# Keys spread over heads by activations instead of transfers, and a new order of the steps, in a two-layer attention and mixture kernel

## The chip, the cores and the metric

The kernel runs on one core of one Trainium2 chip. The metric is the time of one execution on the device, in microseconds. A core has a matrix engine (PE), a vector engine (DVE), a scalar engine (ACT), GpSimd (POOL), and SyncE (SP), which here issues the transfers. Each runs its own instruction stream in order; they wait for each other by semaphores.

## The reference

The input is 16 images of 64 x 64 pixels with 64 features. Four blocks follow each other, each added to its input, except that the last adds only to the tokens that it chose:

```python
# 1: attention over the 16 images, at each pixel
zn = layernorm(z)
q, k, v = (zn @ W).reshape(n, l, l, H=8, C=16) for Wq, Wk, Wv
g = sigmoid(zn @ Wg + bg)
att = softmax(einsum('iabhc,jabhc->ijabh', q, k) / sqrt(C), axis=1)
out = (einsum('ijabh,jabhc->iabhc', att, v) * g) @ Wo + bo
# 2: the two best of 8 experts for each token
top_p, top_i = top_k(softmax(x @ router_w + router_b), 2);  top_p /= sum(top_p)
out = sum over the two of top_p * (x @ expert_w[e] + expert_b[e])
# 3: a convolution gated by a moving average along one image axis
s = s * 0.9 + xi * 0.1
out = (sigmoid(...) * ...) @ W_con + b_con
# 4: 32 experts choose their top 8 tokens; gelu network of 256; scatter add
```

## The kernel before

The pixels are cut into 32 columns of four tiles, 128 tiles of 256 tokens in all, each with its two halves of 64 features on the 128 partitions. Blocks 1 to 3 and the scores of block 4 run in one software pipeline over the tiles. Each engine runs a function `step(i, q)` once in a slot, for column i and quarter q; `slots` (L244) calls it first for some columns written out (`PEELED`, 4), then in a hardware loop with four slots in its body, then for the slots that drain the pipeline. After the loop comes a tail for block 4 (from L1018), which the change does not touch.

The table `LAG` (L32) says how many slots after a tile's start each operation works on it. The order of the operations in an engine's `step` is the engine's program order, so the order of the code and the table together set the order of the work. `TURNS`, `BANK` and `READ_BY` (L52) say which of the eight PSUM banks each group of matmuls on PE writes, in which order, and who reads it last; from them `last_reads` (L205) works out whom PE waits for before it writes a bank again.

The operations that the prediction speaks of, in the order in which a tile passes through them:

- SP loads the tile's input (`x_load`, L269). PE sums it into position (`x_rotate`, L683); squares, statistics and a power -1/2 on POOL (`rstd_att`, L383) give the normalization, which PE spreads (`spread_att`, L745) and DVE multiplies (`z_att`, L952).
- PE projects queries, keys, gate and values (L767, L772, L780, L787). ACT writes the queries to `q_own` (`q_mask`, L557) and copies the keys to `k_sb` (`k_copy`, L564). SP then moves the keys of each head, 16 rows, into one of four copies in `k4` (`k_heads`, L305, eight transfers), so that in each copy the rows of the other heads of a half stay zero. The matmuls of the scores (L648) take `q_own` and `k4`.
- The softmax: maximum and difference on DVE (L889, L895), exponential on ACT (L502), sum and reciprocal on DVE (L916, L920), the probabilities on POOL (`probs`, L393), their transposition on DVE (L964). PE multiplies the values (L807). Even and odd heads are put together by ACT (`even_heads`, L595) and DVE (`odd_heads`, L876), gated (L884), multiplied by the output weights (`att_out`, L666), and added to the input (`x1`, L904).
- The routing of a whole column runs once in four slots: logits on POOL (`router_logits`, with the power on L402), the search for the two largest on DVE (`two_largest`, L973 to L993), `second_exp` on ACT, `gate_ratio` on DVE (L1009), `gates` on POOL (L425 to L434), `gates_T` on PE (L658).
- The gates go through memory: SP stores them, and `gates_load` (L297) spreads them over the partitions in six transfers, for each half one of 1 row, one of 48 rows and one of 15 rows; `x1_load` fetches the tokens twice. The gating multiplies both for four pairs of experts, two pairs on DVE (`gated_x_dve`, L1002) and two on POOL (`gated_x_pool`, L415). PE mixes the experts (`mix`, L692), DVE adds (`x2`, L927).
- The convolution (L708, L814, L912, L760), its residual (`x3`, L959), the output (`out_rotate`, L796, `x3_store`), and the normalized scores of block 4 (`stat_pick`, `spread_pick`, `pick`, L675).

## Time and profile before

| | us |
|---|---|
| three runs | 3241.89, 3265.34, 3272.22 |
| median | 3265.34 |
| the profiled execution | 3251.39 |
| its span | 3249.6 |
| busy in the span: PE, DVE, POOL, ACT | 2340.6, 1619.6, 1384.7, 1142.4 |

The profile is of one execution; its mean granted clock of PE is 0.807 of full speed. A row of a view by line has the engine, the operation, what it writes and reads, the shapes, the number of instructions, then the busy time in us, the mean of one in ns, and the idle time of the engine just before these instructions with what ended it. A row of the timeline begins with the start and the duration in us; in square brackets stands the idle time before it. SPq is SP's queue in its time of issuing. Buffer numbers and halves are left out of names, so `k` is `k4` and `x` may be `x1` or `x3`.

### The profile page before, as it was taken

Reading aid. Unit: us, or ns where it says so; the run is one execution under the profiler, and the core shown is the slowest. Engines: PE = TensorE matmul, PEld = TensorE weight load, DVE = VectorE, ACT = ScalarE, POOL = GpSimd, SP = SyncE. Lnnn points to the kernel's source line nnn. Section 1 sums busy time; section 2 is a strip of 40 time slices with the busy share of each in tenths; the row PEclk is TensorE's granted clock in tenths of the full one; section 3 lists DMA queues with packets and bytes.
Section 4 is the critical chain, followed back from the end, with each engine's and each line's share of the span. In section 5 each row is a group of like instructions: output and inputs, shape, how many; then the busy total and the mean of one; then the engine's idle time right before and its main releaser. Section 6 shows DMA issues by size and latency. Waiting matters only on the chain. (4 is left out here: it accounts for less than half of the span.)

```text
span 3249.6 us, 118532 instructions
## 1 busy us (share of the span) xinstructions
PE 2340.6 (72%) x47804; PEld 1725.9 (53%) x47804; DVE 1619.6 (50%) x2790; ACT 1142.4 (35%) x2652; POOL 1384.7 (43%) x1424
## 2 busy tenths in 40 slices
PE   5668777777777777878777777877777787776270
PEld 4446555555555555555555555555555555554170
DVE  1344555555555555555554555555555555554650
ACT  1233434343333433333333433334333333332300
POOL 2234444444444444444444444444444443444503
PEclk8677888788888878788878888788888888887655
DMA  0144544444444444444444444444444444454300
GB/s 19 45 89 96 107 93 96 93 97 100 95 99 90 100 102 90 96 93 100 95 95 91 99 105 93 96 93 98 100 91 102 88 102 97 94 109 96 70 1 13
DMA packets 231213, 286.39 MB, mean 88 GB/s; under 512 B 37629, under 2 KB 147741, under 8 KB 230749
## 3 DMA queue, kind: packets, MB, share of 16 engines
q1 hardware_dynamic: 228701, 276.87, 40.6%
q8 instruction: 442, 7.24, 1.1%
q0 software_dynamic: 2048, 2.10, 0.2%
q14 instruction: 22, 0.18, 0.0%
HBM read 206.47 MB, written 38.80 MB: 75 GB/s over the span
## 5 line engine op out<-in xcount | busy, mean ns | idle before, releaser
L648 PE MATMUL psum<-k,q_own 64*32 64x64 f32 x16384 | 259.3, 294 | 515.2 <-issue 383.3
L383 POOL TENSOR_TENSOR rstd_att<-var_att,minus_half 128x4 f32<-128x4 f32 x128 | 129.1, 1009 | 1108.5 <-ACT var_att L513 1108.5
L415 POOL TENSOR_TENSOR gated_x<-spread_gates,x_twice 128x512 f32<-128x512 f32 x256 | 402.1, 1591 | 393.7 <-DMA spread_gates<-gates_scratch 393.6
L648 PEld LDWEIGHTS psum<-k,q_own 64*32 64x32 f32 x16384 | 226.5, 137 | 572.7 <-issue 572.7
L1002 DVE TENSOR_TENSOR gated_x<-spread_gates,x_twice 128x512 f32<-128x512 f32 x256 | 270.1, 1096 | 162.0 <-DMA spread_gates<-gates_scratch 162.0
L889 DVE TENSOR_REDUCE smax<-psum 128x32 f32<-128x512 f32 x128 | 88.2, 689 | 490.7 <-PE psum L648 490.6
L807 PE MATMUL psum<-probsT,v_sb 32*32 32x64 f32 x16384 | 226.5, 229 | 121.1 <-issue 120.6
L485 ACT ACTIVATE picks<-psum,pc 128x128 f32 (+1 forms) x128 | 61.4, 480 | 667.8 <-PE psum L675 667.8
L692 PE MATMUL psum<-gated_x,w_expert 128*64 128x256 f32 x2048 | 280.2, 421 | 8.4 <-POOL gated_x L415 8.4
L807 PEld LDWEIGHTS psum<-probsT,v_sb 32*32 32x32 f32 x16384 | 188.9, 104 | 160.7 <-issue 155.1
L393 POOL TENSOR_TENSOR probs<-weights,own_rec 128x1024 f32<-128x1024 f32 x128 | 247.2, 1932 | 12.3 <-POOL own_rec L387 4.4
L692 PEld LDWEIGHTS psum<-gated_x,w_expert 128*64 128x64 f32 x2048 | 150.5, 153 | 144.6 <-issue 96.4
L916 DVE TENSOR_REDUCE ssum<-weights 128x32 f32<-128x512 f32 x128 | 87.8, 686 | 209.1 <-ACT weights L502 209.1
L595 ACT ACTIVATE even_o<-psum,b_all,odd_even 128x512 f32<-128x512 f32 x128 | 99.7, 779 | 170.0 <-PE psum L807 170.0
L964 DVE STREAM_TRANSPOSE probsT<-probs 128x1024 f32<-128x1024 f32 x128 | 158.0, 1235 | 2.5 <-POOL probs L393 2.5
L876 DVE SCALAR_TENSOR_TENSOR both_o<-psum,odd_even,even_o 128x512 f32<-128x512 f32 x128 | 95.7, 748 | 105.7 <-ACT even_o L595 105.6
L666 PE MATMUL psum<-gated_o,w_o 128*64 128x256 f32 x512 | 143.2, 660 | 0.5 <-DVE gated_o L884 0.5
L367 POOL TENSOR_TENSOR rstd_conv<-var_conv,minus_half 128x4 f32<-128x4 f32 x128 | 138.0, 1078 | 5.1 <-ACT var_conv L544 5.1
L683 PE MATMUL psum<-x_in,h_two 128*128 128x256 f32 x256 | 136.3, 630 | 1.0 <-ACT w_expert L454 1.0
L378 POOL TENSOR_TENSOR rstd_pick<-var_pick,minus_half 128x4 f32<-128x4 f32 x128 | 131.3, 1026 | 9.7 <-PE psum L735 9.7
L946 DVE TENSOR_TENSOR z_pick<-x,psum 128x256 f32<-128x256 f32 x128 | 53.9, 421 | 160.1 <-PE psum L735 160.1
L557 ACT ACTIVATE q_own<-psum,b_all 128x512 f32<-128x512 f32 x128 | 88.0, 687 | 69.1 <-PE psum L772 55.4
(227 smaller groups left out, 5152.3 us busy)
## 6 DMA issues: line engine op xcount, KB each, us to landing
spread_gates<-gates_scratch SPq DMA_DIRECT2D x256, 384.0 KB
k<-k_sb SPq DMA_DIRECT2D x1024, 32.0 KB, 2.0
x_twice<-x_scratch SPq DMA_DIRECT2D x256, 126.0 KB
spread_gates<-gates_scratch SPq DMA_DIRECT2D x256, 120.0 KB
x_in<-in_x_fm SPq DMA_DIRECT2D x128, 128.0 KB, 2.1
x_scratch<-x SPq DMA_DIRECT2D x128, 128.0 KB, 1.7
x_back<-x_scratch SPq DMA_DIRECT2D x128, 128.0 KB
out_x<-x_tok SPq DMA_DIRECT2D x128, 128.0 KB, 1.8
```

What stands on the lines that cost most here:

```text
L367: g.tensor_tensor(rstd["conv"][:], var["conv"][:], minus_half[:, 0:4], ALU.pow).then_inc(done["rstd_conv"], 1)
L378: g.tensor_tensor(rstd["pick"][:], var["pick"][:], minus_half[:, 0:4], ALU.pow).then_inc(done["rstd_pick"], 1)
L383: g.tensor_tensor(rstd["att"][:], var["att"][:], minus_half[:, 0:4], ALU.pow).then_inc(done["rstd_att"], 1)
L393: g.tensor_tensor(probs[:], weights[:].unsqueeze(2).broadcast_to([P, 32, 2, N]), own_rec[:].unsqueeze(3).broadcast_to([P, 32, 2, N]), ALU. ...
L415: ins = g.tensor_tensor(gated_x[:, p, :], spread_gates[z % 2][:, p, :], x_twice[z % 2][:], ALU.mult)
L648: ins = t_.matmul(bk2("scores")[g * 32:(g + 1) * 32, r, t * 64:(t + 1) * 64], q_own[rows, c * 512 + tok:c * 512 + tok + 32], k4[rows, :, t ...
L666: ins = t_.matmul(bk("att_out")[b * D:(b + 1) * D, 0:TOK], w_o[:], og, tile_position=(0, b * D))
L683: t_.matmul(bk("x_rotate")[:, 0:TOK], h_two[:], x_in[z % 2][:]).then_inc(done["x_rotate"], 1)
L692: ins = t_.matmul(bk("mix")[b * D:(b + 1) * D, 0:TOK], w_expert[:, p, :], gated_x[:, p, b * TOK:(b + 1) * TOK], start=(p == 0), stop=(p == ...
L807: ins = t_.matmul(dst[:, :, t, :], v_sb[z % 2][g * 32:(g + 1) * 32, t, k * 32:(k + 1) * 32], probsT[g * 32:(g + 1) * 32, first:first + 2, ...
L964: v.transpose(probsT[:].rearrange("p m i -> p (m i)"), probs[:].rearrange("p m t n -> p (m t n)")).then_inc(done["probs_T"], 1)
L1002: ins = v.tensor_tensor(gated_x[:, p, :], spread_gates[z % 2][:, p, :], x_twice[z % 2][:], ALU.mult)
```

## The change

1. The keys. Four activations `mask_keys(m)` on ACT write the four copies in `k4` straight from PSUM, with a scale that is 1 on the rows of the copy's heads and 0 on the others (`head_of`), and the bias times the same (`b_keys`). One stands before `q_mask`, three behind. `k_sb`, `k_copy`, the eight transfers and the setting of `k4` to zero are gone; two small instructions in the setup make the scale and the bias.
2. `x_load` stays at the start and all that follows has a lag at least one higher, so a tile is loaded a slot ahead of its use. The largest lag is 14 instead of 12, and five columns are written out instead of four.
3. `gates_load` has three transfers: 63 rows for each half, and one for the two first rows.
4. All four multiplications of the gating are on DVE; `gated_x_pool` is gone.
5. `LAG`, the banks and the order in every engine's `step` are new. On SP, the store of `x1` and of the output now stand ahead of `gates_store`, `x1_load` and `gates_load`. `last_reads` names each reader once.

```diff
-LAG = {"x_load": 0, "x_rotate": 0, "x_copy": 0, "square_att": 0, "stat_att": 0,
...
+LAG = {"x_load": 0, "x_rotate": 1, "x_copy": 1, "square_att": 1, "stat_att": 1,
...
-PEELED = 4
+PEELED = 5
...
+            head_of, b_keys = cb("head_of", [P, 4]), cb("b_keys", [P, 4])
...
-            k_sb = cb("k_sb", [P, 512])
...
                     lag = LAG["gates_load"]
                     if runs(i, q, lag):
                         z, c = par(q, lag), column(i, q, lag)
-                        wait_apart(sp, (s_gates, c * 16 + 16), (done["gated_x_dve"], at(i, q, lag + 2)), (done["gated_x_pool"], at(i, q, lag + 2)))
+                        wait_apart(sp, (s_gates, c * 16 + 16), (done["gated_x_dve"], at(i, q, lag + 2)))
+                        by_pair = gates_dram[c, :, z].rearrange("k (p x) t -> k x p t", x=2)
                         for e2 in range(2):
-                            per_pair = gates_dram[c, :, z].rearrange("k (p x) t -> k x p t", x=2)[:, e2]
-                            for k, row, rows in ((0, 0, 1), (1, 1, 48), (1, 49, 15)):
-                                dst = spread_gates[z % 2][e2 * D + row:e2 * D + row + rows]
-                                sp.dma_start(dst, per_pair[k].unsqueeze(0).broadcast_to([rows, 4, 512])).then_inc(s_spread[z], 16)
-                    lag = LAG["k_heads"]
-                    if runs(i, q, lag):
-                        z = par(q, lag)
-                        sp.wait_ge(done["k_copy"], at(i, q, lag))
-                        wait(sp, done["scores"], at(i, q, lag + 1))
-                        for h in range(H):
-                            rows = slice(h * C, (h + 1) * C)
-                            sp.dma_start(k4[rows, h % 4, :], k_sb[rows, :]).then_inc(s_k4[z], 16)
...
+                            sp.dma_start(spread_gates[z % 2][e2 * D + 1:(e2 + 1) * D],
+                                         by_pair[1, e2].unsqueeze(0).broadcast_to([D - 1, 4, 512])).then_inc(s_spread[z], 16)
+                        sp.dma_start(spread_gates[z % 2][0:P:D], by_pair[0]).then_inc(s_spread[z], 16)
...
+                def mask_keys(m):
+                    return s.activation(k4[:, m, :].rearrange("p (b t) -> p b t", b=2), bk2("q_proj")[:, :, TOK:2 * TOK],
+                                        ACT.Identity, bias=b_keys[:, m:m + 1], scale=head_of[:, m:m + 1])
...
+                    lag = LAG["k_mask"]
+                    if runs(i, q, lag):
+                        act.wait_ge(done["k_proj"], at(i, q, lag))
+                        wait(act, done["scores"], at(i, q, lag + 1))
+                        for m in range(1, 4):
+                            ins = mask_keys(m)
+                        ins.then_inc(done["k_mask"], 1)
...
+                    lag = LAG["gated_x_dve"]
+                    if runs(i, q, lag):
+                        z, c = par(q, lag), column(i, q, lag)
+                        dve.wait_ge(s_spread[z], c * 48 + 48)
+                        dve.wait_ge(s_x1b[z], c * 48 + 48)
+                        wait(dve, done["mix"], at(i, q, lag + 1))
+                        for p in range(4):
+                            ins = v.tensor_tensor(gated_x[:, p, :], spread_gates[z % 2][:, p, :], x_twice[z % 2][:], ALU.mult)
+                        ins.then_inc(done["gated_x_dve"], 1)
```

On PE, before, from the query projection (L767) to the scores (L648) in the loop; `psum` is the bank written, and the rows L767, L772 and L780 are queries, keys and gate:

```order
L767 MATMUL psum<-z_att,w_all 128x256 x2
L772 MATMUL psum<-z_att,w_all 128x256 x2
L780 MATMUL psum<-z_att,w_all 128x256 x2
L787 MATMUL psum<-w_all,z_att 128x128 x4
L796 MATMUL psum<-h_two,x3_3 128x128 x2
L807 MATMUL psum<-probsT,v_sb1 32x2x32 x64
L814 MATMUL psum<-z_conv,w_prim 128x256
L815 MATMUL psum<-z_conv,w_scan 128x256
L181 ISA
L648 MATMUL psum<-k4,q_own 32x64 x64
```

After, on PE, the same stretch, from L756 (queries) to L655 (scores):

```order
L756 MATMUL psum<-z_att,w_all 128x256 x2
L761 MATMUL psum<-z_att,w_all 128x256 x2
L769 MATMUL psum<-z_att,w_all 128x256 x2
L776 MATMUL psum<-w_all,z_att 128x128 x4
L783 REGISTER_ALU
L786 MATMUL psum<-gated_x,w_expert 64x256 x8
L795 MATMUL psum<-gated_o,w_o 64x256 x2
L803 MATMUL psum<-ident,rstd_conv 64x128 x4
L634 MATMUL psum<-h_two,x3_0 128x128 x2
L642 MATMUL psum<-ident,rstd_pick 64x128 x4
L655 MATMUL psum<-k4,q_own 32x64 x64
```

The values (L807) and the expansion (L814, L815) have moved out of this stretch; the mix (L786), the attention's output (L795) and two spreads have moved into it.

On ACT, before, what stands around the copy of the keys (L564):

```order
L544 ACTIVATE var_conv<-psum,eps 128x4
L551 ACTIVATE square_pick<-x3_3 128x256
L557 ACTIVATE q_own<-psum,b_all 128x16x2x16
L178 ISA
L564 ACTIVATE k_sb<-psum,b_all 128x512
L571 ACTIVATE gate0<-psum,b_all 128x2x4x64
L579 COPY v_sb0<-psum 128x512
```

After, on ACT, the keys written to `k4` (L442):

```order
L561 ACTIVATE picks<-psum,pc 128x2x16x4
L567 ACTIVATE var_pick<-psum,eps 128x4
L442 ACTIVATE k4<-psum,b_keys,head_of 128x512
L579 ACTIVATE q_own<-psum,b_all 128x16x2x16
L442 ACTIVATE k4<-psum,b_keys,head_of 128x512 x3
L451 ACTIVATE gate1<-psum,b_all 128x2x4x64
L459 COPY v_sb1<-psum 128x512
```

One key copy has become four activations, one of them ahead of the queries; gate and values still follow.

On DVE, before, the end of a slot with the gating (L1002) and the beginning of the next:

```order
L959 SCALAR_TENSOR_TENSOR x3_3<-psum,b_all,x2_3 128x256
L964 STREAM_TRANSPOSE probsT<-probs 128x1024
L998 ISA
L1002 TENSOR_TENSOR gated_x<-spread_gates0,x_twice0 128x512 x2
L876 SCALAR_TENSOR_TENSOR both_o<-psum,odd_even,even_o 128x512
L884 SCALAR_TENSOR_TENSOR gated_o<-gate1,both_o 128x512
L889 TENSOR_REDUCE smax<-psum 128x32
```

After, on DVE, the gating (L939) and what follows it, in the slot that ends with the search for the two largest and `x1` (rows of the search left out behind its first):

```order
L927 TENSOR_REDUCE ssum<-weights 128x32
L931 RECIPROCAL srec<-ssum 128x32
L939 TENSOR_TENSOR gated_x<-spread_gates0,x_twice0 128x512 x4
L944 REGISTER_ALU
L946 TENSOR_TENSOR z_att<-xr2,psum 128x256
L950 SCALAR_TENSOR_TENSOR both_o<-psum,odd_even,even_o 128x512
L958 SCALAR_TENSOR_TENSOR x3_3<-psum,b_all,x2_3 128x256
L963 STREAM_TRANSPOSE probsT<-probs 128x1024
L970 SCALAR_TENSOR_TENSOR gated_o<-gate0,both_o 128x512
L979 TENSOR_REDUCE r_m1<-r_lg 128x16
```

The gating has moved from the slot's end to the place ahead of `z_att`; the search (from L979) is now followed by `x1` (L1007), which stood ahead of it.

## Rows read from the trace of the kernel before

**Rows 1.** Window's length; PE, PEld, DVE, ACT, POOL busy (instructions); PEclk; DMA share; GB/s.
```profile
1000.00:2000.00 1000.00, 763.62 (x16215) 559.17 (x16214) 524.54 (x904) 383.64 (x904) 449.26 (x444) 0.84 0.46 96
```
**Rows 2.** Groups by line and form, 1000 to 2600 us, PE.
```profile
L648 PE MATMUL psum<-k,q_own 64*32 64x64 f32 x9088 | 143.1, 293 | 278.9 <-issue 192.8 <-DMA k<-k_sb 86.0
...
L807 PE MATMUL psum<-probsT,v_sb 32*32 32x64 f32 x8960 | 123.4, 226 | 69.4 <-issue 69.3
```
**Rows 3.** Timeline, 1499 to 1550 us: two scores, and the keys between.
```profile
1505.30 1.52 PE L648 MATMUL psum<-k,q_own 64*32 64x64 f32 x128 [3.36 <-issue]
...
1521.29 0.68 ACT L564 ACTIVATE k_sb<-psum,b_all 128x512 f32<-128x512 f32 x1
1522.00 5.67 SPq L305 DMA_DIRECT2D k<-k_sb  x8
...
1524.46 0.59 PE L815 MATMUL psum<-z_conv,w_scan 128*128 128x256 f32 x2
...
1529.23 2.04 PE L648 MATMUL psum<-k,q_own 64*32 64x64 f32 x128 [4.17 <-issue]
```
**Rows 4.** The page, DMA issues: number, size of one, us to landing.
```profile
spread_gates<-gates_scratch SPq DMA_DIRECT2D x256, 384.0 KB
k<-k_sb SPq DMA_DIRECT2D x1024, 32.0 KB, 2.0
```
**Rows 5.** Windows of 2 us around the wait of rows 3; columns as in rows 1.
```profile
1527.00:1529.00 2.00, 0.00 (x0) 0.00 (x0) 0.84 (x1) 0.00 (x0) 2.00 (x4) 0.52 0.31 81
...
1531.00:1533.00 2.00, 2.00 (x41) 0.89 (x23) 1.65 (x3) 0.00 (x0) 0.00 (x0) 0.50 0.59 178
...
1535.00:1537.00 2.00, 2.00 (x23) 1.28 (x19) 1.32 (x3) 1.23 (x4) 0.15 (x1) 1.00 0.57 161
```
**Rows 6.** Groups by line and form, 1000 to 2600 us, POOL, DVE, ACT.
```profile
L415 POOL TENSOR_TENSOR gated_x<-spread_gates,x_twice 128x512 f32<-128x512 f32 x141 | 221.0, 1587 | 204.6 <-DMA spread_gates<-gates_scratch 204.6
...
L1002 DVE TENSOR_TENSOR gated_x<-spread_gates,x_twice 128x512 f32<-128x512 f32 x140 | 147.7, 1096 | 84.5 <-DMA spread_gates<-gates_scratch 84.5
...
L393 POOL TENSOR_TENSOR probs<-weights,own_rec 128x1024 f32<-128x1024 f32 x70 | 135.2, 1932 | 6.9 <-POOL own_rec L387 2.9
...
L595 ACT ACTIVATE even_o<-psum,b_all,odd_even 128x512 f32<-128x512 f32 x70 | 54.6, 779 | 93.4 <-PE psum L807 93.4
...
L402 POOL TENSOR_TENSOR r_rstd<-r_var,minus_half 128x16 f32<-128x16 f32 x18 | 52.2, 2901 | 1.5
...
L889 DVE TENSOR_REDUCE smax<-psum 128x32 f32<-128x512 f32 x71 | 48.9, 689 | 266.8 <-PE psum L648 266.7
```
**Rows 7.** Timeline, 1575 to 1600 us: mix, projection, search, gates.
```profile
1578.52 1.95 PE L692 MATMUL psum<-gated_x,w_expert 128*64 128x256 f32 x16
...
1586.02 0.60 PE L780 MATMUL psum<-z_att,w_all 64*128 64x256 f32 x4
...
1588.99 0.29 DVE L973 TENSOR_REDUCE r_m<-r_lg 128x16 f32<-128x128 f32 x1 [2.20 <-POOL r_lg L407]
...
1598.53 0.66 PE L658 MATMUL psum<-ident,gates 128*128 128x128 f32 x2 [2.44 <-POOL gates L434]
```
**Rows 8.** Tile spread_gates, 1000 to 2600 us: least, median, longest in ns.
```profile
L1002 DVE TENSOR_TENSOR gated_x<-spread_gates,x_twice x140: 681/693/1768, 1021.2 to 2594.0; 128x512 f32<-128x512 f32 x140
```
**Rows 9.** Timeline, 1499 to 1550 us: a power on POOL and a product on DVE.
```profile
1515.86 1.01 POOL L383 TENSOR_TENSOR rstd_att<-var_att,minus_half 128x4 f32<-128x4 f32 x1 [4.64 <-ACT var_att L513]
...
1516.45 0.42 DVE L940 SCALAR_TENSOR_TENSOR gated_prim<-ema_t,prim 128x256 f32<-128x256 f32 x1
```
**Rows 10.** Windows of 1 us with spread traffic and with little; columns as in rows 1.
```profile
1583.00:1584.00 1.00, 1.00 (x18) 0.83 (x17) 0.26 (x1) 0.32 (x2) 1.00 (x1) 1.00 1.07 148
1570.00:1571.00 1.00, 1.00 (x34) 0.86 (x28) 0.16 (x1) 0.39 (x1) 1.00 (x1) 1.00 0.31 70
1571.00:1572.00 1.00, 0.45 (x3) 0.05 (x1) 0.58 (x1) 0.90 (x3) 1.00 (x2) 1.00 0.20 45
```
**Rows 11.** Timeline of PE, 1640 to 1710 us, where the loop's body begins again.
```profile
1643.53 1.58 PE L648 MATMUL psum<-k,q_own 64*32 64x64 f32 x92 [2.13 <-issue]
```

More of the change, by code:

```diff
@@ L217, in last_reads @@
                         for reader in READ_BY[u]:
-                            count = column(i, slot, lag) + 1 if u in BATCHED else at(i, slot, lag)
-                            if (reader, back) not in [f[2] for f in found]:
-                                found.append((done[reader], count, (reader, back)))
+                            if reader not in found or back < found[reader][0]:
+                                count = column(i, slot, lag) + 1 if u in BATCHED else at(i, slot, lag)
+                                found[reader] = (back, done[reader], count)
                         break
-                return [(s_, count) for s_, count, _ in found]
+                return [(s_, count) for _, s_, count in found.values()]
             def bank_free(pe, i, q, name):
@@ L437, in _ @@
+                    lag = LAG["rstd_pick"]
+                    if runs(i, q, lag):
+                        pool.wait_ge(done["var_pick"], at(i, q, lag))
+                        wait(pool, done["spread_pick"], at(i, q, lag + 1))
+                        g.tensor_tensor(rstd["pick"][:], var["pick"][:], minus_half[:, 0:4], ALU.pow).then_inc(done["rstd_pick"], 1)
                 slots(pool, step)
@@ new lines, in step @@
+                    lag = LAG["x_copy"]
+                    if runs(i, q, lag):
+                        z = par(q, lag)
+                        act.wait_ge(done["x_rotate"], at(i, q, lag))
+                        wait(act, done["x1"], at(i, q, lag + 4))
+                        s.copy(xr[z][:], bk("x_rotate")[:, 0:TOK]).then_inc(done["x_copy"], 1)
+                    lag = LAG["score_exp"]
+                    if runs(i, q, lag):
+                        act.wait_ge(done["score_sub"], at(i, q, lag))
+                        s.activation(weights[:], weights[:], ACT.Exp, scale=float(C) ** -0.5).then_inc(done["score_exp"], 1)
@@ new lines, in step @@
+                    lag = LAG["square_att"]
+                    if runs(i, q, lag):
+                        z = par(q, lag)
+                        act.wait_ge(done["x_copy"], at(i, q, lag))
+                        wait(act, done["stat_att"], at(i, q, lag + 1))
+                        s.activation(square["att"][:], xr[z][:], ACT.Square).then_inc(done["square_att"], 1)
+                    lag = LAG["route_copy"]
+                    if runs(i, q, lag):
+                        z = par(q, lag)
+                        act.wait_ge(done["route"], at(i, q, lag))
+                        wait(act, done["router_logits"], column(i, q, lag))
+                        s.copy(raw[:, 4 * z:4 * z + 4, :].rearrange("p x e -> p (x e)"), bk("route")[:, 0:36]).then_inc(done["route_copy"], 1)
@@ new lines, in step @@
+                    lag = LAG["gates_copy"]
+                    if begins(i, q, lag):
+                        c = column(i, q, lag)
+                        act.wait_ge(done["gates_T"], c + 1)
+                        wait(act, s_gates, c * 16)
+                        s.copy(gates_rows[:].rearrange("p k t -> p (k t)"), bk("gates_T")[:, 0:2 * P]).then_inc(done["gates_copy"], 1)
+                    lag = LAG["var_conv"]
+                    if runs(i, q, lag):
+                        act.wait_ge(done["stat_conv"], at(i, q, lag))
+                        wait(act, done["rstd_conv"], at(i, q, lag + 1))
+                        s.activation(var["conv"][:], bk("stat_conv")[:, 0:4], ACT.Identity, bias=eps[:, 1:2],
+                                     scale=1.0 / D).then_inc(done["var_conv"], 1)
@@ L591, in step @@
+                    lag = LAG["square_pick"]
+                    if runs(i, q, lag):
+                        z = par(q, lag)
+                        act.wait_ge(done["x3"], at(i, q, lag))
+                        wait(act, done["stat_pick"], at(i, q, lag + 1))
+                        s.activation(square["pick"][:], x3[z][:], ACT.Square).then_inc(done["square_pick"], 1)
                     lag = LAG["even_heads"]
@@ L885, in step @@
+                    lag = LAG["z_pick"]
+                    if runs(i, q, lag):
+                        z = par(q, lag)
+                        dve.wait_ge(done["spread_pick"], at(i, q, lag))
+                        wait(dve, done["pick"], at(i, q, lag + 2))
+                        v.tensor_tensor(z_pick[z % 2][:], x3[z][:], bk("spread_pick")[:, 0:TOK], ALU.mult).then_inc(done["z_pick"], 1)
                     lag = LAG["score_max"]
```

658 lines of the change are left out of this document (294 added, 364 removed).

## Prediction

> **What bounds the kernel now.** The loop over 32 columns of four steps takes nearly all of the time, so I read the middle of the span first. In a stretch of 1000 us the scores line has 9088/1600 of its matmuls per us; at 128 in a step, 9088 are 71 steps in 1600 us, or 22.54 us a step [rows 1, 2]. 128 steps are 2885 us; the other 366 us of the execution's 3251 are setup, filling, draining and the tail, which the change leaves alone. In 44.4 steps PE is busy 763.62 us, 17.2 a step; VectorE has 11.8, GpSimd 10.1, ScalarE 8.6 [rows 1]. No engine is full, so the step is a chain of waits with PE in most of it.
>
> The reader is then to look at which wait on PE is longest. Before the scores 278.9 us stand idle, 3.9 a step; inside the values 69.4, 1.0 a step; the other lines share the remaining 0.4 [rows 2]. The timeline shows what the scores wait for: ScalarE ends the copy of the keys at 1521.97, SP then needs 5.67 us to issue eight small transfers, the last of them lands 2.0 us after its issue, and PE, done with the expansion at 1525.05, starts the scores at 1529.23 [rows 3, 4]. "Issue" as the releaser means here that the wait stood on an earlier instruction of PE's queue.
>
> The wait has a second price. While PE stands, the granted clock goes from 1.00 to 0.52 (the lower of 2.4 and 1.2 GHz), is still 0.50 when PE is full again, and is back at 1.00 four microseconds later [rows 5]. The mean clock of 0.84 [rows 1] means 0.16/0.5 = 32% of the time at the lower level: 7.2 us a step, of which some 2.7 are idle and 4.5 are PE working at half speed. Those 4.5 would be 2.25 at full clock: PE's own work is 15.0 us a step.
>
> **The keys.** Eight transfers of 32 KB a step [rows 4] and one copy of 0.68 us [rows 3] go. In their place stand four ScalarE activations from PSUM with a scale and a bias by pointer. The nearest row is the even heads' copy, the same shape with a pointer scale and a pointer bias: 0.779 us [rows 6]. So ScalarE has 8.6 - 0.68 + 4 x 0.78 = 11.0 us a step. After the key projection the chain is one mask, the query mask (0.68, as the key copy), three masks: 0.78 + 0.68 + 2.34 = 3.8 us. By the new order PE has behind the key projection: gate and value projections (0.6 each), the mix (1.95), and four groups of 0.6 to 0.7 [rows 7]: 5.7 us. So the keys are hidden by 1.9 us, if ScalarE is free when the projection ends; the gate's tanh and the value copy stand behind the masks in its queue, and their readers come a slot later. If the cover is gone, because ScalarE is late by 3 us, the step pays 1.1.
>
> **The gating.** GpSimd loses two multiplications of 1.587 us, VectorE gets two more [rows 6]. VectorE's price is 0.693 in the median, 0.681 at least, 1.768 at most, 1.096 in the mean [rows 6, 8]: two levels, and I take the low one four times, with one instruction delayed by the largest excess, 1.768 - 0.693 = 1.08, when GpSimd's probabilities (1.93 us [rows 6]) run beside it: 3.84 us a step. Bounds: 4 x 0.68 = 2.7 and 4 x 1.1 = 4.4. VectorE then has about 13, GpSimd 6.9 a step: neither is full, but the four stand in VectorE's queue ahead of the normalized input of attention, which the projections wait for. From the end of the scores that chain is: maximum 0.69 [rows 6], difference as much, exponential 0.78 (as the even heads), sum 0.69, reciprocal 0.25 (my choice for a small instruction), gating 3.84, normalization 0.42 (as the same shape in [rows 9]), and five hand-overs that I put at 0.2: 8.35 us. PE meanwhile does what lies between scores and projections: 15.0 less 1.5 of scores at full clock [rows 3] and less the 6.9 from the query projection to the slot's end (three projections' worth 1.8, value 0.6, mix 1.95, four groups 2.6), that is 6.6, plus 1.0 of gaps in the values: 7.6. So PE waits 0.75 at the query projection; with the bounds of the gating and hand-overs of nothing this lies between 0 and 1.4.
>
> What I weigh there is whether the small GpSimd powers delay VectorE as well. A VectorE multiplication of two SBUF operands took its whole 0.42 us inside a power of 1.01 us on GpSimd [rows 9], so I charge them nothing. The Trainium skill (SBUF — State Buffer, "SBUF: two separate sides") says that the two engines take a shared port pair by turns, for a whole instruction. This trace agrees for the wide operations (two levels of price) and not for that pair. By the rule for every pair the step would be about 1 us longer, and the time near 2880.
>
> **Transfers.** SP issues 8 fewer for the keys and 3 fewer for the gates, 20.25 to 9.25 a step. The 384 KB spreads of 48 rows [rows 4] and the smaller ones of 15 and 1 become two of 63 rows (8 KB each, 504 KB) and one small one. Where spread transfers run, the engines' share is 1.07 at 148 GB/s [rows 10], so the 128 rows of a step, 1.05 MB, take 7.1 us. The new shape, 63 rows in one transfer, has no row. Bounds: 7.1 us (same rate), and the rates of thinner mixes, 70 and 45 GB/s [rows 10]: 15.0 and 23.3 us. I take the first, the row nearest in size. The first two fit into a step, and the fetch is issued a slot before its use; the slower two are rivals D and F.
>
> A page speaks against this part: the Trainium skill (DMA: Bandwidth & Descriptors, "Why a DMA increments its semaphore by 16 and not by 1") says that a transfer uses as many engines as the largest number up to 16 that divides its outer dimension. By it 63 rows use 9 engines, and at 148/16 = 9.3 GB/s an engine the two large transfers, 112 KB for each engine, take 12 us; the column's first fetch could then be 5.2 us late, a time of at most 2920. No run here shows it yet.
>
> **The column's stops.** Once in four steps the routing chain runs. In the new order the residual of attention is issued behind the two-largest search, which waits for GpSimd's router logits with a power of 2.9 us [rows 6], and the scores of the next slot wait for that residual's bank. Before, the search stood idle 2.2 us at its first instruction [rows 7]. I put 1.8 on it. The gates' transposition waited 2.44 us for GpSimd [rows 7]; I keep 1.3 of it. At the loop's end PE stopped 2.13 us within the scores [rows 11]: 1.8 (as half of the steps looked at had less). Together 4.9, or 1.2 a step.
>
> **Sum.** 15.0 of PE at full clock + 1.0 of gaps in the values + 0.75 at the projections + 0.5 of small waits (some of them where a statistic is now close behind its square) + 1.2 = 18.45 us a step. Saved: 22.54 - 18.45 = 4.09, times 128 = 523. 3251 - 523 = 2728; draining is two slots deeper (+10), a memset goes (-2): 2736. The profiled execution lies 14 under the median of the three runs (3265): 2750 us.
>
> **Rivals.**
> A, the forecast: 17.3 to 19.3 us a step, 2600 to 2860. For it: the largest idle time has one cause, which is removed, and the clock follows. Against it: the chain is near to PE's work everywhere.
> B, PE alone: the waits at the projections and of the column vanish in the slack of a slot: 15.0 + 1.0 + 0.4 = 16.4, 2099 + 366 + 24 = 2490. For it: no other engine has over 13 us. Against it: the routing chain and the loop's end stop PE today as well.
> C, VectorE's loop bounds: scores, softmax, gating, normalization, projections, masks and scores again form one ring, since VectorE keeps order. Its length: 2.1 of three wide reductions, 0.78, 0.25, gating at 4.4, 0.42, projections 1.2, masks 3.8, scores 1.5 = 14.45, ten hand-overs 2.0, and 1.93 + 1.0 of GpSimd's probabilities and one power in its way: 19.4; with about 1.1 of the column's stops 20.5, so 2624 + 366 + 24 = 3014. For it: the mean of 1.096 today. Against it: half of GpSimd's gating traffic, which makes that mean, goes.
> D, slower: the spread in 63-row transfers moves at 45 GB/s, 23.3 us a step, and the other loads share its engines. Their part: the mean share of 0.46 [rows 1] is 10.4 us of all engines a step, less 7.1 for the gates and, at the same rate, 1.8 for the keys' 0.26 MB: 1.5. So 24.8 a step, 2.26 x 128 = 289 more than today, 3554 beside the median. It decides from about 50 GB/s on (21.0 + 1.5 = 22.5, no gain). For it: no such shape in the trace. Against it: today's transfers move at three times that rate.
> E, no change: the wait moves from transfers to ScalarE's masks, because ScalarE, in order, reaches them late behind pick and statistics. It would have to be 6 us late at each step, while it is idle 11 of 22: about 3260.
> F, the column's first fetch late: at 70 GB/s the spread lands 7.9 us later, and only the first of a column's four fetches follows its gates closely: 7.9/4 = 2.0 a step, 20.45, 3006. For it and against it: as for D, at a nearer row.
>
> **Chances.** A 0.52, B 0.14, C 0.17, D 0.06, E 0.04, F 0.07. The time is A's, 2750. The range: from 2480, which leaves out the lower half of B, to 3040, which holds F, and C but for its upper end; left out are E and D, half of B, and a little of C, together about 0.2. A measurement of this kernel can tell about 1% from no change. Faster by over 1%: A, B, C and F, 0.90. Within 1%: E, 0.04. Slower: D, 0.06.
>
> **What would show it.** Right: the scores' idle time near nothing and never put down to a transfer; the granted clock at 0.95 or more in the loop; 18 to 19 us from scores to scores; a mask near 0.78; the gating between 0.69 and 1.0; most of PE's remaining idle time ahead of the query projection, the gates' transposition and, each fourth step, the scores. Wrong: gating that waits for spread gates at each step (D), a gating mean near 1.1 with PE waiting 3 us at the query projection (C), scores that wait for masks (E), or a clock that still falls to 0.5 at each step, which would return the 2.25 us though the wait is gone.

## Result: 1% slower, and the profile after

The changed kernel takes 3294.23 us (median of 4 runs, 3290.57 to 3298.23), the kernel before 3267.82 beside it: a ratio of 1.0101, 95% interval 1.0054 to 1.0148. The forecast was 2750, in a range from 2480 to 3040, with 0.90 for faster. It lies outside.

The wait that the change was to remove is gone. What took its place shows in one table, PE's waits from 1000 to 2600 us of the changed kernel (line waited at, what ended the wait; total us, times, longest):

```profile
PE psum L730 <- issue: 125.0, 33, 6.0
PE psum L715 <- issue: 115.0, 35, 6.4
PE psum L634 <- issue: 34.7, 17, 2.3
PE psum L655 <- issue: 22.0, 17, 1.7
```

L715 are the values, L730 the pick, L634 the output's rotation at the head of a slot, L655 the scores. Before, 278.9 us stood ahead of the scores and 69.4 in the values [rows 2]; now the scores have 22.0 and never wait for the keys or for ScalarE, and some 240 us stand in the values and just behind them. All of it is "issue": time in which PE waited for nothing that the profile shows.

The window that answers to [rows 1], with the same columns:

```profile
1000.00:2000.00 1000.00, 804.42 (x15498) 631.34 (x15500) 487.32 (x957) 450.98 (x991) 327.72 (x341) 0.73 0.28 81
```

From 1000 to 2600 us there are 8576 matmuls of the values, 128 in a step (rows below): 67 steps of 23.9 us; before it was 22.54. At a busy share of 0.804 PE works 19.2 us a step, where the forecast had 15.0; the clock is 0.73 of full in the mean, not 0.95 or more. The groups that answer to [rows 2] and [rows 6], 1000 to 2600 us:

```profile
L442 ACT ACTIVATE k<-psum,b_keys,head_of 128x512 f32<-128x512 f32 x272 | 196.9, 785 | 119.2 <-PE psum L761 119.2
L939 DVE TENSOR_TENSOR gated_x<-spread_gates,x_twice 128x512 f32<-128x512 f32 x268 | 170.6, 695 | 0.0
...
L387 POOL TENSOR_TENSOR probs<-weights,own_rec 128x1024 f32<-128x1024 f32 x67 | 141.0, 2104 | 0.0
L715 PE MATMUL psum<-probsT,v_sb 32*32 32x64 f32 x8576 | 129.5, 246 | 118.6 <-issue 115.0 <-ACT gates_rows L523 1.9
...
L382 POOL TENSOR_TENSOR rstd_att<-var_att,minus_half 128x4 f32<-128x4 f32 x67 | 96.0, 1433 | 13.4 <-ACT var_att L534 12.9
```

A mask of the keys takes 0.785 us, a gating multiplication 0.695, both as priced. One slot of the changed kernel, in order of time:

```profile
1535.10 0.74 SPq L300 DMA_DIRECT2D spread_gates<-gates_scratch  x2
...
1536.35 1.84 PE L715 MATMUL psum<-probsT,v_sb 32*32 32x64 f32 x126
...
1542.25 0.37 PE L715 MATMUL psum<-probsT,v_sb 32*32 32x64 f32 x2 [4.05 <-issue]
...
1546.30 1.22 PE L756 MATMUL psum<-z_att,w_all 64*128 64x256 f32 x4
```

PE stops 126 matmuls into the values, two before their end. No wait is written there in the code: all 128 belong to one loop that starts when its inputs are there. Then everything behind is late, and the projections of the same shape take 1.22 us instead of 0.60 [rows 7], at the lower clock. In windows of 1 and 2 us (the clock is the third column from the end) that slot shows:

```profile
1537.00:1538.00 1.00, 1.00 (x83) 0.95 (x66) 1.00 (x2) 0.37 (x2) 1.00 (x2) 0.57 0.23 80
...
1539.00:1541.00 2.00, 0.00 (x0) 0.00 (x0) 0.00 (x0) 0.00 (x0) 2.00 (x2) 0.50 0.60 207
...
1549.00:1551.00 2.00, 2.00 (x16) 1.43 (x14) 0.00 (x0) 2.00 (x5) 0.00 (x0) 0.55 0.00 0
1551.00:1553.00 2.00, 2.00 (x26) 1.35 (x22) 0.09 (x1) 1.84 (x4) 0.00 (x0) 1.00 0.00 0
```

It falls inside the values, about 1 us before the stop, while PE is still busy; it stays at 0.50 through the stop and is back some 8 us after PE is at work again. One column shows where the stops lie. From PE's timeline, the rows behind a stop:

```profile
1224.37 1.78 PE L655 MATMUL psum<-k,q_own 64*32 64x64 f32 x105 [1.66 <-issue]
...
1236.59 0.43 PE L715 MATMUL psum<-probsT,v_sb 32*32 32x64 f32 x6 [2.06 <-issue]
...
1258.39 0.37 PE L715 MATMUL psum<-probsT,v_sb 32*32 32x64 f32 x2 [3.51 <-issue]
...
1283.95 0.67 PE L730 MATMUL psum<-z_pick,w_pick 128*32 128x64 f32 x16 [6.01 <-issue]
...
1306.05 0.66 PE L730 MATMUL psum<-z_pick,w_pick 128*32 128x64 f32 x11 [3.76 <-issue]
```

The next column, 95 us later, has the same five: 105 matmuls, 6, 2, 16 and 11 are left behind the stops each time. A sixth stands once a column ahead of the rotation (L634), where the loop's body begins again. What lies between two of them, from the windows view (length; PE's matmuls and weight loads with their numbers in brackets; VectorE, ScalarE, GpSimd; clock; transfers):

```profile
1224.37:1236.59 12.22, 10.06 (x251) 9.03 (x250) 5.79 (x12) 3.48 (x10) 6.02 (x8) 0.50 0.16 45
1236.59:1258.39 21.80, 18.05 (x372) 14.26 (x373) 10.49 (x19) 10.47 (x23) 7.12 (x8) 0.73 0.40 128
1258.39:1283.95 25.56, 19.39 (x373) 14.86 (x373) 10.48 (x19) 11.31 (x24) 6.37 (x7) 0.77 0.31 81
1283.95:1306.05 22.10, 18.19 (x375) 14.34 (x374) 10.48 (x19) 10.55 (x23) 7.04 (x6) 0.81 0.26 75
```

Matmuls and weight loads are instructions of their own: 501, 745, 746 and 749. This view leaves out waits and register instructions; with them the trace has 512, 768, 768 and 768 records of PE from one of these places to the next. So the stops are bound to the code's position, in multiples of 256, not to any operation. That led to theory S: **PE runs dry of instructions.** Its instruction stream arrives in pieces of 256; a piece that is fetched while PE is inside a dense stretch (values and scores have 256 instructions each, done in about 2 us or less) comes too late, later still when bulk transfers run beside it. The rival, theory P: PE waits for a semaphore that the profile does not show, that of GpSimd's power for the normalization, which now runs beside the gating.

The Trainium skill (Runtime: NRT & Kernel Launch, "Instruction fetch mechanics") says that an engine's instructions are brought in by its own DMA queue in blocks of 256, the next one while the present one runs, and that this is mostly hidden. The distances agree with the 256; "mostly hidden" does not hold here.

### The profile page after: what moved, and what is told of

The parts are those of the page before. It is cut to its first block and busy times, and to the rows that moved or that the text cites. A ratio compares the mean times of both kernels' runs of the same rounds, so it can differ in the third digit from the quotient of the medians.

```text
span 3290.2 us, 116556 instructions
## 1 busy us (share of the span) xinstructions
PE 2499.9 (76%) x47804; PEld 1970.1 (60%) x47804; DVE 1571.4 (48%) x3048; ACT 1396.4 (42%) x3036; POOL 1065.7 (32%) x1167
## 5 line engine op out<-in xcount | busy, mean ns | idle before, releaser
L442 ACT ACTIVATE k<-psum,b_keys,head_of 128x512 f32<-128x512 f32 x512 | 370.7, 785 | 245.5 <-PE psum L761 245.5
L376 POOL TENSOR_TENSOR own_rec<-srec,odd_even 128x64 f32<-128x64 f32 x128 | 77.2, 603 | 1140.9 <-DVE srec L931 1140.9
L946 DVE TENSOR_TENSOR z_att<-xr,psum 128x256 f32<-128x256 f32 x128 | 53.9, 421 | 748.1 <-PE psum L739 748.1
L715 PE MATMUL psum<-probsT,v_sb 32*32 32x64 f32 x16384 | 244.1, 247 | 212.2 <-issue 205.5
L715 PEld LDWEIGHTS psum<-probsT,v_sb 32*32 32x32 f32 x16384 | 197.4, 111 | 238.0 <-issue 225.9
L939 DVE TENSOR_TENSOR gated_x<-spread_gates,x_twice 128x512 f32<-128x512 f32 x512 | 328.7, 701 | 11.4 <-DMA spread_gates<-gates_scratch 11.4
L786 PE MATMUL psum<-gated_x,w_expert 128*64 128x256 f32 x2048 | 300.8, 444 | 8.9 <-DVE gated_x L939 8.9
L730 PE MATMUL psum<-z_pick,w_pick 128*32 128x64 f32 x2048 | 97.0, 299 | 208.2 <-issue 208.2
L1007 DVE SCALAR_TENSOR_TENSOR x<-psum,b_all,xr 128x256 f32<-128x256 f32 x128 | 61.9, 484 | 402.8 <-PE psum L795 402.4
L655 PE MATMUL psum<-k,q_own 64*32 64x64 f32 x16384 | 209.7, 240 | 56.0 <-issue 38.5
L655 PEld LDWEIGHTS psum<-k,q_own 64*32 64x32 f32 x16384 | 182.3, 111 | 85.9 <-issue 85.8
L786 PEld LDWEIGHTS psum<-gated_x,w_expert 128*64 128x64 f32 x2048 | 160.4, 164 | 118.6 <-issue 72.9
L730 PEld LDWEIGHTS psum<-z_pick,w_pick 128*32 128x32 f32 x2048 | 60.0, 142 | 283.9 <-issue 283.9
L561 ACT ACTIVATE picks<-psum,pc 128x128 f32 (+1 forms) x128 | 61.2, 478 | 346.1 <-PE psum L730 346.1
L382 POOL TENSOR_TENSOR rstd_att<-var_att,minus_half 128x4 f32<-128x4 f32 x128 | 179.3, 1401 | 43.3 <-ACT var_att L534 42.7
L495 ACT ACTIVATE prim<-psum,pc 128x256 f32<-128x256 f32 x128 | 60.5, 473 | 270.6 <-PE psum L665 270.5
L756 PE MATMUL psum<-z_att,w_all 64*128 64x256 f32 x512 | 154.3, 697 | 7.9 <-DVE z_att L946 7.4
```

Of the source, the lines that this page charges most:

```text
L382: g.tensor_tensor(rstd["att"][:], var["att"][:], minus_half[:, 0:4], ALU.pow).then_inc(done["rstd_att"], 1)
L442: return s.activation(k4[:, m, :].rearrange("p (b t) -> p b t", b=2), bk2("q_proj")[:, :, TOK:2 * TOK], ACT.Identity, bias=b_keys[:, m:m + ...
L655: ins = t_.matmul(bk2("scores")[g * 32:(g + 1) * 32, r, t * 64:(t + 1) * 64], q_own[rows, c * 512 + tok:c * 512 + tok + 32], k4[rows, :, t ...
L715: ins = t_.matmul(dst[:, :, t, :], v_sb[z % 2][g * 32:(g + 1) * 32, t, k * 32:(k + 1) * 32], probsT[g * 32:(g + 1) * 32, first:first + 2, ...
L730: ins = t_.matmul(bk("pick")[j * EP:(j + 1) * EP, b * 64:(b + 1) * 64], w_pick[:, b, :], zs, tile_position=(0, j * EP))
L756: t_.matmul(bk2("q_proj")[:, b, 0:TOK], w_all[rows, 0, :], z_att[rows, :], tile_position=(b * D, 0))
```

## Experiments

Ratios are to the kernel before on the same chip, with 95% intervals.

**1. Another shape of the gates' spread.**

```diff
-                            sp.dma_start(spread_gates[z % 2][e2 * D + 1:(e2 + 1) * D],
-                                         by_pair[1, e2].unsqueeze(0).broadcast_to([D - 1, 4, 512])).then_inc(s_spread[z], 16)
-                        sp.dma_start(spread_gates[z % 2][0:P:D], by_pair[0]).then_inc(s_spread[z], 16)
+                            for k, row, rows in ((0, 0, 1), (1, 1, 48), (1, 49, 15)):
+                                dst = spread_gates[z % 2][e2 * D + row:e2 * D + row + rows]
+                                sp.dma_start(dst, per_pair[k].unsqueeze(0).broadcast_to([rows, 4, 512])).then_inc(s_spread[z], 16)
```

Expected: 

> The changed kernel with the gates spread again in six transfers of 48, 15 and 1 rows; all else as in the changed kernel. Theory S (the stalls of PE in the values and the pick are instructions that come late, because the bulk transfers of 63 rows hold the DMA engines, about 9 of 16 busy, through that stretch): the transfers finish sooner (engines' share near 1 instead of 0.6), the stalls fall from 3.6 us a step to 1 to 2.5, the clock rises, time 2950 to 3150 us. Theory P (the stalls are a semaphore wait on GpSimd's power for the normalization, which runs beside the gating): nothing changes, 3260 to 3330 us.

Measured: 3242.2 us, ratio 0.9977 (0.9954 to 1.0000). From 1000 to 2600 us the pick and the values still lose 118.2 and 110.3 us. The mean share of the engines rose from 0.28 to 0.42, so the shape does decide how many of them work, but not how long PE stands. The time lies between the two forecasts. My expectation under S was wrong in this: the shape of the transfers hardly counts.

**2 and 3. Loads at another time, and no spread at all.** The second run adds one wait ahead of the load of x1:

```diff
                     lag = LAG["x1_load"]
                     if runs(i, q, lag):
                         z, c = par(q, lag), column(i, q, lag)
+                        wait_apart(sp, (done["pick"], at(i, q, LAG["pick"])))
```

Expected: 

> The changed kernel with SP's loads of x1 and of the gates (still 63 rows) held back until PE has done the pick of the same slot, so that they run beside the projections and the mix. Theory S: the stalls in values and pick fall under 1 us a step; some late landing at the gating or in the scores may take their place; 2750 to 3000 us. Theory P: the stalls stay at 3 us or more a step, 3260 us or more.

Measured: 3052.31 us, ratio 0.9391 (0.9369 to 0.9414). The third leaves out the two large spread transfers and takes a constant in their place:

```diff
-                        for e2 in range(2):
-                            sp.dma_start(spread_gates[z % 2][e2 * D + 1:(e2 + 1) * D],
-                                         by_pair[1, e2].unsqueeze(0).broadcast_to([D - 1, 4, 512])).then_inc(s_spread[z], 16)
...
+                for z in range(2):
+                    setup(g.memset(spread_gates[z][:], 0.25))
```

Expected: 

> The changed kernel without the two large spread transfers: the gates of the token features are a constant, only the 16 KB transfer of the two bias rows is left. This leaves out 1 MB of traffic a step. Theory S: stalls in values and pick under 1.5 us a step (the x1 load is still there), clock over 0.9, 2550 to 2850 us. Theory P: 3250 us or more, stalls as in the changed kernel.

Measured: 3018.03 us in its one run. PE's waits of the run with held loads, 1000 to 2600 us, and of the one without the spread:

```profile
PE psum L716 <- issue: 74.0, 38, 2.6
PE psum L635 <- issue: 70.3, 19, 7.3
PE psum L731 <- issue: 39.4, 37, 1.9
```
```profile
PE psum L714 <- issue: 77.7, 37, 2.5
PE psum L729 <- issue: 44.2, 38, 1.7
PE psum L633 <- issue: 40.6, 19, 2.5
```

Values and pick (the two lines are moved by one or two) lose 113 and 122 us instead of 240. With the held loads the rotation's wait rises from 34.7 to 70.3 us. Theory P, under which nothing should move, falls; but with 1 MB less in a step the stops are still there, half as long, and the clock is still 0.74 to 0.75. Both times lie above what I expected. So traffic is half of it.

**4. The keys alone, in the kernel before.**

```diff
-                        for h in range(H):
-                            rows = slice(h * C, (h + 1) * C)
-                            sp.dma_start(k4[rows, h % 4, :], k_sb[rows, :]).then_inc(s_k4[z], 16)
...
+                        for m in range(4):
+                            ins = s.activation(k4[:, m, :].rearrange("p (b t) -> p b t", b=2), bk2("q_proj")[:, :, TOK:2 * TOK],
+                                               ACT.Identity, bias=b_keys[:, m:m + 1], scale=head_of[:, m:m + 1])
+                        ins.then_inc(done["k_copy"], 1)
```

Expected: 

> The kernel before with the keys alone changed: four ScalarE activations write the masked copies, the eight transfers are gone; order, lags and gate transfers as before. If the wait for the scores was the key transfers, as the prediction says, it shrinks from 3.9 us a step to under 1.5 and the clock rises: 2650 to 2950 us. If that wait was something else (instructions that come late there too), it stays above 3 us: 3150 us or more.

Measured: 3137.95 us, ratio 0.9664 (0.9637 to 0.9690), between the two. PE's waits, 1000 to 2600 us, 73 steps:

```profile
PE psum L799 <- ACT k L555: 152.7, 74, 2.3
PE psum L640 <- issue: 116.6, 70, 4.0
```

Ahead of the scores (L640) 1.6 us a step are left of 3.9, close to the forecast 1.5, and what is left is "issue". From 1000 to 2600 us the clock rises only from 0.83 to 0.86. And in this order the values (L799) write the PSUM banks that the masks read, and wait 2.1 us a step for the last of the four. The keys on ScalarE are a gain by themselves; in the new order, which puts other work behind the projections, PE never waits for the masks from 1000 to 2600 us.

**5 to 8. The code's position.** These runs put waits on a semaphore that has long been reached ahead of PE's first step; two of them make one instruction (the trace then has 128 more records of PE for 256 waits):

```diff
                 pe.wait_ge(s_dve_setup, N_DVE_SETUP)
+                for _ in range(256):
+                    pe.wait_ge(s_weights, 32)
```

Expected, changed kernel and 128 instructions: 

> The changed kernel with 128 instructions that do nothing put into PE's stream ahead of its first step (256 waits on a semaphore that has long been reached), so that the code of the loop stands 128 instructions later; order, transfers and work are the same. In the changed kernel the stalls stand at fixed places of the code, whole multiples of 256 PE instructions apart. Theory S: the places where PE runs dry move by 128 instructions, from the end of the values to their middle, so that no stretch between two of them is the values alone; the stalls fall to under 2 us a step, 2800 to 3100 us. Theory P (a semaphore wait on GpSimd): the stalls stay where they are, between values and pick; 3260 to 3330 us.

Measured: 2798.3 us, ratio 0.8595 (0.8537 to 0.8654). Nothing that does any work differs from the changed kernel. Its PE waits, 1000 to 2400 us, 73 steps, with L717 the values, L657 the scores, L636 the rotation:

```profile
PE psum L636 <- issue: 59.5, 18, 4.5
PE psum L657 <- issue: 45.5, 27, 2.2
...
PE psum L717 <- issue: 0.6, 3, 0.2
```

The stops in the values are 0.6 us where they were 115 (in 1600 us); the pick's row is gone.

Expected, 256 instructions: 

> The changed kernel with 256 instructions that do nothing ahead of PE's first step instead of 128. Theory S: the places where PE runs dry are 256 instructions apart, so they return to where they were, at the end of the values and before the pick; 3260 to 3330 us, as the changed kernel. If the instructions help in another way (time at the start, a later start of PE): 2750 to 2850 us, as with 128.

Measured: 3326.35 us, ratio 1.0225 (1.0182 to 1.0268), at the upper end of the expectation. The stops are back at the same matmuls as in the changed kernel, 6, 2 and 16 left:

```profile
1245.62 0.43 PE L717 MATMUL psum<-probsT,v_sb 32*32 32x64 f32 x6 [2.74 <-issue]
...
1267.78 0.37 PE L717 MATMUL psum<-probsT,v_sb 32*32 32x64 f32 x2 [3.78 <-issue]
...
1290.55 0.67 PE L732 MATMUL psum<-z_pick,w_pick 128*32 128x64 f32 x16 [3.30 <-issue]
```

This is the run that settles it: 128 instructions that do nothing take 15% away, 256 give it back.

Expected, 128 instructions and the loads held until the pick: 

> The same 128 instructions, and the loads of x1 and of the gates held back until the pick. Theory S: neither short stretches nor traffic beside them, stalls under 0.7 us a step apart from the loop's end; clock over 0.9; 2550 to 2800 us. If the two cures act on the same thing and the rest is something else: 3000 to 3060 us, as the held loads alone.

Measured: 2742.08 us, ratio 0.8427 (0.8379 to 0.8475), 2% better than without the hold. What remains is mostly the rotation, 78.2 us in 18 turns of the loop. The stops fell as theory S said, to 12.0 us in the values and the scores together; the clock did not rise over 0.9 but is 0.85 from 1000 to 2400 us.

Expected, 64 instructions and the loads held: 

> The loads held back, and 64 instructions instead of 128. Theory S: the places move to about 180 matmul and weight instructions into the values and to the start of the scores; the stretch before the second is the long one; 2600 to 2950 us. Otherwise 3000 to 3060 us.

Measured: 3297.31 us in its one run, far off. I had the second place wrong: it is not at the start of the scores but near their end (121 of their 128 matmuls are ahead of it), so a piece is again a dense stretch almost alone. Two of its rows, 7 matmul records of the scores and 29 of the values behind a stop:

```profile
1231.83 0.31 PE L658 MATMUL psum<-k,q_own 64*32 64x64 f32 x7 [1.77 <-issue]
...
1262.42 0.52 PE L718 MATMUL psum<-probsT,v_sb 32*32 32x64 f32 x29 [1.94 <-issue]
```

Expected, the kernel before and 128 instructions: 

> The kernel before with the same 128 instructions ahead of PE's first step. There the places lie in the first half of the values and of the scores, and move to the last quarter of both; the second lies behind the wait for the keys, which gives the fetch time. Theory S: 3230 to 3330 us, within 2% of before; the stalls in the scores and values change place. If instructions that do nothing made a kernel faster in themselves, it would show here: under 3150 us.

Measured: 3349.98 us, ratio 1.0296 (1.0238 to 1.0354): the instructions help nothing in themselves. It is slower by more than the 2% that I allowed. In the kernel before a stop, once a column, had 92 of the 128 matmul records of the scores behind it [rows 11]; now, in several steps of a column, 20 or 22, and of the values 15 or 16:

```profile
1267.58 0.34 PE L809 MATMUL psum<-probsT,v_sb 32*32 32x64 f32 x16 [0.74 <-issue]
...
1275.58 0.64 PE L650 MATMUL psum<-k,q_own 64*32 64x64 f32 x22 [2.29 <-issue]
```

**9. A version that beats both.** As the run with 128 instructions and held loads, but in a column's last slot the loads go at once, because the code of the loop's start is fetched right behind it:

```diff
+                        if q != 3:
+                            wait_apart(sp, (done["pick"], at(i, q, LAG["pick"])))
```

Expected: 

> As the run with 128 instructions and the loads held until the pick, but in the last slot of a column the loads are not held, so that they are further on when PE fetches the code of the loop's start again. There PE stood up to 7.6 us in each turn of the loop. Theory S: that stand falls by 2 us or more a turn, 2650 to 2730 us. If the stand at the loop's start has nothing to do with the loads: 2735 to 2760 us, or more where the values of the last slot now run dry.

Measured: 2724.46 us, ratio 0.8368 (0.8334 to 0.8402), the fastest of all. By its ratio it lies 0.7% under the run that holds all loads, on another chip, and the two intervals overlap, so the time alone does not show this gain. The rotation's wait is 57.3 us in 18 turns instead of 78.2: 1.2 us a turn, less than the 2 expected.

**10. The gating's part.** In the version with 128 instructions, two of the four multiplications go back to GpSimd:

```diff
-                        for p in range(4):
+                        for p in range(2):
...
+                    lag = LAG["gated_x_pool"]
+                    if runs(i, q, lag):
...
+                        for p in range(2, 4):
+                            ins = g.tensor_tensor(gated_x[:, p, :], spread_gates[z % 2][:, p, :], x_twice[z % 2][:], ALU.mult)
+                        ins.then_inc(done["gated_x_pool"], 1)
```

Expected: 

> The changed kernel with the 128 instructions, and two of the four gating multiplications back on GpSimd, behind the probabilities. It tests the gating's part of the change where PE no longer runs dry at the values. Theory G (the division between the engines costs nothing on the path, but the two engines slow each other): VectorE's multiplication rises from 0.70 to 1.0 us or more, GpSimd's is 1.6; GpSimd's power for the convolution comes 3 us later and PE, which waited for it already in some steps, waits longer: 2800 to 2900 us. Theory N (the gating's place is free): 2780 to 2820 us.

Measured: 2907.57 us, ratio 0.8926 (0.8895 to 0.8957), 3.9% above the version without it. The place of the wait is another than theory G had: PE's mix waits for GpSimd's gating itself, 2.9 us in 31 steps. Both multiplications rose less than theory G had, to 0.746 and 1.276 us, and the time is just over its range. PE has one more wait in each step here, so the code's position is not quite the same: the stops in the scores rise from 45.5 to 61.2 us, those at the rotation fall from 59.5 to 15.2.

```profile
PE psum L798 <- POOL gated_x L409: 89.0, 31, 5.2
```
```profile
L409 POOL TENSOR_TENSOR gated_x<-spread_gates,x_twice 128x512 f32<-128x512 f32 x140 | 175.8, 1276 | 0.0
...
L951 DVE TENSOR_TENSOR gated_x<-spread_gates,x_twice 128x512 f32<-128x512 f32 x140 | 98.7, 746 | 0.0
```

## Why the prediction was wrong, and where it was right

**The step that failed** is the one that priced PE's own supply: "1.0 of gaps in the values" and "1.8 at the loop's end" were taken over from the trace of before as if they were properties of those operations. They were properties of the code's position. In the changed kernel the stops measured (118.6 + 125.0 + 34.7 + 22.0)/67 = 4.5 us a step, where the sum had 1.0 and 1.8/4. Rows to see it were there: a stop with 36 matmul records of the scores before it and 92 behind it [rows 11] is no semaphore, since nothing is waited for in the midst of these matmuls. The stops in the values of before were alike; in the two columns from 1640 us six of eight steps have one, with 75 to 84 records behind it:

```profile
1658.99 1.05 PE L807 MATMUL psum<-probsT,v_sb 32*32 32x64 f32 x84 [1.65 <-issue]
...
1679.97 1.19 PE L807 MATMUL psum<-probsT,v_sb 32*32 32x64 f32 x80 [1.89 <-issue]
```

**The fetch is in the trace.** The profile's DMA view of the changed kernel has a queue of kind "instruction" with 440 packets of 16 KB in the span. Its rows for the four stretches between the five stops, in order:

```profile
q8 instruction: 2, 0.03, 1.2%
...
q8 instruction: 3, 0.05, 1.1%
...
q8 instruction: 3, 0.05, 0.9%
...
q8 instruction: 3, 0.05, 1.6%
```

They hold 512, 768, 768 and 768 records of PE: one packet for each 256. The times of the packet ahead of each stop's end, in us:

| PE stands from | packet from | packet to | PE goes on |
|---|---|---|---|
| 1222.71 | 1221.50 | 1222.78 | 1224.37 |
| 1234.53 | 1233.70 | 1235.02 | 1236.59 |
| 1254.88 | 1255.29 | 1256.98 | 1258.39 |
| 1277.94 | 1281.35 | 1282.57 | 1283.95 |
| 1302.29 | 1301.06 | 1304.33 | 1306.05 |

Each time PE goes on 1.4 to 1.7 us after a packet has come in. From 1000 to 2600 us this holds for all 84 stops of over 0.6 us in the values, the pick and the scores (1.1 to 1.7 us). In 15 turns of the loop, its return left out, each of 165 blocks of 256 records has exactly one packet (with the return a turn has 14), which begins 0.6 to 8.6 us after PE has entered the block, 2.4 in the median; with the loads held (experiment 2) the median is 1.15. So here the next piece comes only while the present one runs, and a present one that is nearly all values or scores is over first.

**The clock.** The step "PE's own work is 15.0 us", at full clock, became 19.2. The stops are one part of that: with 128 instructions, and nothing else changed, PE is busy 1240.83/73 = 17.0 us a step at a clock of 0.84 from 1000 to 2400 us, instead of 0.73. The other 2.0 us stay when the stops are gone. In the run with 128 instructions and held loads the clock still falls in the midst of the values, after 33 us in which PE never stood for more than 0.15 us:

```profile
1240.00:1242.00 2.00, 2.00 (x98) 1.39 (x92) 2.00 (x4) 1.50 (x3) 2.00 (x3) 0.65 0.04 8
1242.00:1244.00 2.00, 2.00 (x26) 1.27 (x25) 0.14 (x2) 0.48 (x1) 1.92 (x2) 0.50 0.00 0
```

Of its 74 falls from 1000 to 2400 us, 31 have no stop of over 0.6 us within 4 us, and 21 of these begin in the values. So the prediction's reading that the low clock came from PE's standing, and would go with it, failed too; in no run here did the loop reach 0.95.

Together 19.2 + 4.5 and 0.2 of small waits are 23.9, the step measured from 1000 to 2600 us (1600/67). Against the 18.45 forecast PE's own work added 4.2 and the stops 3.05 (4.5 in place of 1.0 and 1.8/4), and the other terms, 2.0, came to next to nothing.

That a step is some 5% longer (23.9 us against 22.5 to 22.9, by the scores and the values of [rows 2]) and the kernel only 1% goes back to the columns that are written out. From 99.78 to 234.19 us the scores start 16.8 us apart in the mean (8 steps, the later stages not all running yet); before, from 105.98 to 282.88 us, 22.1. The changed kernel has five such columns and 27 in the loop, the kernel before four and 28. That it is the code's position, which differs there from slot to slot, is not shown.

**Right: the keys.** 0.785 us a mask against 0.78; hidden behind the projections and the mix; ScalarE at 10.8 us a step against 11.0. Alone they give 3.4%, less than the wait's size: in experiment 4 the values wait for the masks instead, and the clock hardly rises.

**Right: the gating's price,** 0.695 a multiplication, at the low level. What I charged for contention fell on the other side: VectorE was not held up, GpSimd's power beside it rose from 1.01 [rows 9] to 1.43 us and its probabilities from 1.93 [rows 6] to 2.10. So the rule of the Trainium skill (SBUF — State Buffer, "SBUF: two separate sides") that I set aside for the small powers agrees with what GpSimd shows, though the power grew by 0.42 us, less than one multiplication; no run separates the port from other causes. The 0.75 us at the query projection did not come: in the version with 128 instructions no wait for the normalized input is among those listed.

**Right: the spread is not the bound.** VectorE's gating waited 11.4 us in all for it. By the Trainium skill (DMA: Bandwidth & Descriptors, "Why a DMA increments its semaphore by 16 and not by 1") its 63 rows use nine engines of sixteen. The trace comes near that: the share was 0.60, or 9.6 engines, from 1539 to 1541 us, while mostly the spread ran. So D and F fell, and E too, as nothing waits for the masks. None of the rivals named PE's instructions as a resource.

**With the supply out of the way the total comes near, in part by luck.** The version with 128 instructions needs 1400/73 = 19.2 us a step and 2798 us, the best one 2724, against 18.45 and 2750. The terms are not right: PE was still busy for 17.0 us a step instead of 15.0, and its waits came to 2.2 instead of 3.45, so two errors cancel in part.

**Open.** Why the packet begins 0.6 us after PE enters a block in one place and 8.6 in another: the bulk loads are a part of it, as the held loads show, but what else is not known. Why the clock falls in the values without a stop. A loop of two columns, which would halve the turns at which the rotation waits, was not tried.

## What to carry to other kernels

A wait of PE that the profile puts down to "issue", in the midst of a group of matmuls and with the same count behind it in every turn of a loop, is a place in the code: count the instructions between two of them, and look in the DMA view for packets of the instruction queue, before believing in a semaphore. Where a loop has dense stretches of small matmuls, a few instructions that do nothing, ahead of the loop, are a cheap test, and a change of order is not judged until it has been measured at more than one position. Bulk loads did less harm here when held back to a sparse stretch of PE.

## What was not expected of the hardware

The same work in the same order took 3294 or 2798 us by the position of PE's loop in its code, a difference larger than that of the whole change. In the changed kernel the load of x, 128 KB, took 8.3 us from issue to landing, and the store of the gates 3.7, with the new order and the new spread; before they took 2.1 and 1.9:

```profile
x_in<-in_x_fm SPq DMA_DIRECT2D x128, 128.0 KB, 8.3
...
gates_scratch<-gates_rows SPq DMA_DIRECT2D x32, 128.0 KB, 3.7
```
